# A graph layer with attention and experts: the order of the steps between its two phases is rewritten, and the ring of gathered messages is made six groups deep

## The reference

```python
xn = _layernorm(x)                                   # [6250, 256]
# graph part: 100000 edges sorted by dst, 16 relations
transformed = einsum('ni,rio->rno', xn, weight)      # table of node x relation rows
gnn = segment_sum(transformed[rel_type, src] * norm, dst, num_segments=6250)
# linear attention, 8 heads, softmax of k over the nodes
q, k, v = split(xn @ Wqkv);  k = softmax(k, axis=nodes)
mix = (einsum('nhd,hdv->nhv', q, einsum('nhd,nhv->hdv', k, v)) * gate(xn)) @ Wproj + bproj
x = x + gnn + mix
# 8 experts, the best two of a softmax router, each gelu(t @ w1 + b1) @ w2 + b2
t = _layernorm(x)
return x + t + sum_e combine[:, e] * expert_e(t)
```

## Time and profile before

| what | value |
|---|---|
| median of 3 runs | 1624.4 us (1623.64 to 1628.15) |
| the profiled execution | 1619.85 us |
| its span | 1618.1 us |
| PE busy | 1571.3 us (97%) |
| DVE busy | 1338.5 us (83%) |
| POOL busy | 1010.4 us (62%) |
| ACT busy | 966.3 us (60%) |

### The profile page before, as it was taken

How to read it: one execution, slowest core, us unless ns; L and a number is a source line. 1 busy time by engine, 2 the same in 40 slices (tenths; PEclk the granted TensorE clock), 3 DMA queues, 4 the chain that set the end, 5 groups by cost and what they waited for, 6 DMA issues and landing times.

```text
span 1618.1 us, 31745 instructions
## 1 busy us (share of the span) xinstructions
PE 1571.3 (97%) x10509; PEld 1441.1 (89%) x10509; DVE 1338.5 (83%) x3383; ACT 966.3 (60%) x2161; POOL 1010.4 (62%) x1111
## 2 busy tenths in 40 slices
PE   7999999999999999998779999999999999999998
PEld 6888888888888888886669999999999999999998
DVE  7888665588888888874568999999999999999985
ACT  4454322356556656645457776776767776676764
POOL 5533322677777777737457777777777777777620
PEclk9999999999999999999899999999999999999999
DMA  9777656789888888887233333333333333334320
GB/s 300 263 255 259 232 227 238 242 282 284 286 290 273 288 291 275 286 266 248 88 95 108 105 115 103 112 106 118 105 106 108 107 113 102 112 105 118 105 59 10
DMA packets 127076, 290.50 MB, mean 180 GB/s; under 512 B 21271, under 2 KB 49724, under 8 KB 126914
## 3 DMA queue, kind: packets, MB, share of 16 engines
q1 hardware_dynamic: 86068, 177.19, 29.9%
q0 software_dynamic: 39952, 110.13, 25.2%
q10 hardware_dynamic: 894, 1.16, 0.2%
HBM read 149.49 MB, written 138.90 MB: 178 GB/s over the span
## 4 chain that ended last, share of the span: by engine, by line
PE 90%; DVE 3%; issue 2%; ACT 2%; DMA 1%; POOL 1%; SPq 0%; ACTq 0%; DVEq 0%; POOLq 0%
PE bank L1832 71%; PE bank L2036 4%; PE bank L2037 3%; PE bank L1876 2%; PE bank L1877 2%; PE bank L2032 1%; PE bank L1887 1%; PE bank L1988 1%; PE bank L2076 1%; PE bank L2088 1%; DMA xres<-in_L_gnn_weight 1%; PE bank L1842 1%; DVE pad L1262 1%; PE bank L2085 1%; DMA stg<-table,idxcur 0%
## 5 line engine op out<-in xcount | busy, mean ns | idle before, releaser
L830 POOL DMA_INDIRECT stg<-table,idxcur x495 | 543.1, 1097 | 238.5 <-issue 149.1
L1832 PE MATMUL bank<-wreg,xt 128*128 128x512 f32 x2352 | 578.1, 396 | 0.9 <-DVE wreg L1189 0.4
L1832 PEld LDWEIGHTS bank<-wreg,xt 128*128 128x128 f32 x2352 | 432.9, 188 | 88.8 <-ACT stg L872 1.2
L712 POOL DMA_INDIRECT raw<-table,idxa x297 | 302.2, 1018 | 87.7 <-issue 75.9
L1832 PE MATMUL bank<-tt,wreg 128*128 128x256 f32 (+1 forms) x2400 | 321.9, 284 | 2.7 <-DVE tt L1691 2.7
L1832 PE MATMUL bank<-wreg,ht 128*128 128x256 f32 x2352 | 313.5, 282 | 0.2 <-DVE ht L1741 0.2
L1832 PEld LDWEIGHTS bank<-tt,wreg 128*128 128x128 f32 x2400 | 298.7, 191 | 5.8 <-DVE tt L1691 3.1
L1832 PEld LDWEIGHTS bank<-wreg,ht 128*128 128x128 f32 x2352 | 292.4, 189 | 0.4 <-DVE ht L1741 0.4
L1622 DVE SCALAR_TENSOR_TENSOR ml<-stg,nrm,mh 128x256 fp32r<-128x256 f32 x445 | 190.9, 477 | 15.3 <-ACT mh L1044 15.2
L1237 DVE COPY stg<-bank 128x512 f32<-128x512 f32 x196 | 134.0, 686 | 83.9 <-PE bank L1832 82.7
L1044 ACT ACTIVATE mh<-stg,nrm 128x256 fp32r<-128x256 f32 x445 | 196.4, 499 | 0.3 <-PE bank L2037 0.3
(11 more groups left out here) (248 smaller groups left out, 2317.0 us busy)
## 6 DMA issues: line engine op xcount, KB each, us to landing
table<-stg SPq DMA_DIRECT2D x196, 512.0 KB, 3.6
kv_d<-kvs SPq DMA_DIRECT2D x49, 256.5 KB, 4.9
xt_d<-xt SPq DMA_DIRECT2D x49, 256.0 KB, 4.6
xtp<-xt_d SPq DMA_DIRECT2D x24, 512.0 KB, 3.9
stg<-table,idxcur POOLq DMA_INDIRECT x495, 2.9
sk<-kv_d SPq DMA_DIRECT2D x24, 256.5 KB, 5.5
out_x<-xres SPq DMA_DIRECT2D x24, 256.0 KB
xres<-in_x POOLq DMA_DIRECT2D x23, 256.0 KB, 4.1
```

Source lines behind the costliest of these rows:

```text
L712: pool.indirect_dma_start(ring_a[:, r * EARLY + j, :], None, table[0:LIMIT, :], bass.IndirectOffsetOnAxis(ap=idxa[:, at:at + 1], axis=0)). ...
L830: pool.indirect_dma_start(stg[:, (s % 4) * SUP + j, :], None, table, bass.IndirectOffsetOnAxis(ap=idxcur[:, at:at + 1], axis=0)).then_inc( ...
L1832: mm = pe.matmul(dst, stat(a, c), mov(b, c), start=(n == 0), stop=(n == 3 * chunks - 1))
```

## The change

The ring holds six groups instead of four, packed without gaps (ring_at), with six semaphores, and POOL waits for the sums of the group six earlier. The block of indices holds four half pairs instead of two, and a half pair's indices are copied one step later than before for pair 0. The first four groups are split, and the 16 groups after them stay unsplit (WHOLE_GROUPS). The roots of pair 0 are taken one gather later, those of pair 1 two gathers earlier. The mask of the heads is made in setup, as 128 x 4 numbers, and HEADS reads it as a broadcast. Two semaphores are dropped, and QUERY_ROWS counts on another. The list CHANGE is written anew; the steps in it are the same.

```diff
-    ROOTS, EARLIER_ROOTS = (7, 1), {1: (4, 1), 2: (5, 0)}
+    ROOTS, EARLIER_ROOTS = (7, 1), {1: (4, 2), 2: (4, 1)}
...
+    GROUPS_HELD = 6
...
-        idxcur = sb("idxcur", [P, 4 * (EB - EARLY)], I32, two)
+        idxcur = sb("idxcur", [P, 8 * (EB - EARLY)], I32, two)
...
+        heads = small[:, 52:52 + NB]
...
-        gath = [sem(f"gath{g}") for g in range(4)]
+        gath = [sem(f"gath{g}") for g in range(GROUPS_HELD)]
...
-            return S < WHOLE_GROUPS
+            return WHOLE_GROUPS[0] <= S < WHOLE_GROUPS[1]
-            return tiles_before(S) - tiles_before(WHOLE_GROUPS)
+            first, last = WHOLE_GROUPS
+            return tiles_before(S) - (tiles_before(last) - tiles_before(first) if S >= last else 0)
+
+        def ring_at(S, j):
+
+            return tiles_before(S % GROUPS_HELD) + j
...
-            pool.wait_ge(consts, 10)
+            pool.memset(heads, 1.0).then_inc(consts, 1)
+            pool.wait_ge(consts, 11)
+            pool.affine_select(out=heads, in_=heads, compare_op=ALU.is_ge, fill=0.0, base=0,
+                               pattern=[[-HEAD, NB]], channel_multiplier=1).then_inc(consts, 1)
+            pool.wait_ge(consts, 12)
+            pool.affine_select(out=heads, in_=heads, compare_op=ALU.is_ge, fill=0.0, base=HEAD - 1,
+                               pattern=[[HEAD, NB]], channel_multiplier=-1).then_inc(consts, 1)
             pc = Tally(pool_chain)
 
...
                 n = EB - EARLY
-                at = half * 2 * n
+                at = (2 * i + half) % 4 * 2 * n
                 pool.tensor_copy(idxcur[:, at:at + rows * n].rearrange("p (r e) -> p r e", e=n),
                                  g3[:, bass.ds(4 * i + 2 * half, rows), EARLY:EB]).then_inc(idx_cur, 1)
-
-            def heads():
-                by_head = ctxbd.rearrange("p c (h e) -> p c h e", h=NB)
-                pool.memset(ctxbd, 1.0).then_inc(consts, 1)
-                pool.wait_ge(consts, 11)
-                pool.affine_select(out=by_head, in_=by_head, compare_op=ALU.is_ge, fill=0.0, base=0,
-                                   pattern=[[0, CC], [-HEAD, NB], [0, HEAD]], channel_multiplier=1).then_inc(consts, 1)
-                pool.wait_ge(consts, 12)
-                pool.affine_select(out=by_head, in_=by_head, compare_op=ALU.is_ge, fill=0.0, base=HEAD - 1,
-                                   pattern=[[0, CC], [HEAD, NB], [0, HEAD]], channel_multiplier=-1).then_inc(consts, 1)
 
             pool.wait_ge(flag_ready, 1)
             far = pool.value_load(flag[0:1, 0:1], min_val=0, max_val=NT * P * R)
             first_phase_over(pool)
-            heads()
             next_indices(0, 0, 2)
-            next_indices(0, 1, 2)
             for h in range(PIECES):
                 pool.wait_ge(tbl_st[h], 16 * NT)
...
                 for s in range(groups):
                     if s % 4 == 0:
                         pool.wait_ge(idx_cur, 2 * i + s // 4 + 1)
-                    if s >= 4 or not isinstance(i, int) or i > 0:
-
-                        pool.wait_ge(edge_mm, 8 * i + s - 3)
+                    S = 8 * i + s
+                    if S >= GROUPS_HELD:
+                        pool.wait_ge(edge_mm, S - GROUPS_HELD + 1)
                         apart(pool)
                     for j in range(PART[s % 2]):
                         if (s, j) == EARLIER_ROOTS.get(i, ROOTS) and not (isinstance(i, int) and i < 1):
                             roots2(i - 1, 2)
                         if s % 4 == 3 and j == 1:
                             if s == 3:
-                                if not isinstance(i, int) or i > 0:
-                                    next_indices(i, 1, min(2, groups // 2 - 2))
+                                next_indices(i, 1, min(2, groups // 2 - 2))
                             elif groups == 8:
                                 next_indices(i + 1, 0, 2)
-                        at = s // 2 * n + (s % 2) * CUT + j
+                        at = (4 * i + s // 2) % 8 * n + (s % 2) * CUT + j
                         pool.indirect_dma_start(
-                            stg[:, (s % 4) * SUP + j, :], None, table,
+                            stg[:, ring_at(S, j), :], None, table,
                             bass.IndirectOffsetOnAxis(ap=idxcur[:, at:at + 1], axis=0)
-                            ).then_inc(gath[s % 4], 16)
+                            ).then_inc(gath[S % GROUPS_HELD], 16)
 
             def roots2(p, nt):
...
-                act.wait_ge(gath[s % 4], 16 * n * (2 * i + s // 4 + 1))
+                act.wait_ge(gath[S % GROUPS_HELD], 16 * n * (S // GROUPS_HELD + 1))
                 at = EB * (4 * i + s // 2) + EARLY + (s % 2) * CUT
                 if whole(S):
                     for j in range(n):
-                        m = stg[:, (s % 4) * SUP + j, :]
+                        m = stg[:, ring_at(S, j), :]
                         act.activation(m, m, ACT.Copy, scale=nrm[:, bass.ds(at + j, 1)]).then_inc(msg_hi, 1)
                     return
-                act.wait_ge(edge_mm, S - 1)
+                if S < 2:
+                    act.wait_ge(ctx_mm, HELD)
+                else:
+                    act.wait_ge(edge_mm, S - 1)
                 for j in range(n):
-                    act.activation(mh[:, (s % 2) * CUT + j, :], stg[:, (s % 4) * SUP + j, :], ACT.Copy,
+                    act.activation(mh[:, (s % 2) * CUT + j, :], stg[:, ring_at(S, j), :], ACT.Copy,
                                    scale=nrm[:, bass.ds(at + j, 1)]).then_inc(msg_hi, 1)
...
                 for c in range(CC):
-                    dve.scalar_tensor_tensor(out=ctxbd[:, c, :], in0=bank[5][:, c * P:(c + 1) * P], scalar=rden[:, c:c + 1],
-                                             in1=ctxbd[:, c, :], op0=ALU.mult, op1=ALU.mult).then_inc(ctx_done, 1)
+                    dve.scalar_tensor_tensor(
+                        out=ctxbd[:, c, :].rearrange("p (h e) -> p h e", h=NB),
+                        in0=bank[5][:, c * P:(c + 1) * P].rearrange("p (h e) -> p h e", h=NB), scalar=rden[:, c:c + 1],
+                        in1=heads.unsqueeze(2).to_broadcast([P, NB, HEAD]), op0=ALU.mult,
+                        op1=ALU.mult).then_inc(ctx_done, 1)
 
             def CLEAR():
                 dve.memset(halves(c3[:]), 0.0).then_inc(c3_clear, 1)
...
                         pe.wait_ge(msg_hi, done + j + 1)
-                        mm = pe.matmul(bank[u % 2][:, 0:C], halves(sel[:, m, :]), stg[:, (s % 4) * SUP + j, :],
+                        mm = pe.matmul(bank[u % 2][:, 0:C], halves(sel[:, m, :]), stg[:, ring_at(S, j), :],
                                        start=(s % 2 == 0 and j == 0), stop=(s % 2 == 1 and j == PART[1] - 1))
                         continue
...
                 if isinstance(p, int) and p == 0:
-                    pe.wait_ge(wqc_done, 1)
+                    pe.wait_ge(ctx_done, 2 * CC + 2)
 
                 for v in range(CC):
...
 
-WHOLE_GROUPS = 20
+WHOLE_GROUPS = (4, 20)
 
 
...
 CHANGE = (
-    "HELD_ROWS", "ROWS_OF 0", "FADE", "SELECT 0 0", "SELECT 0 1", "SHIFT 2", "EXP 2", "ROWS_OF 1", "MSGS 0 0", "SUMS 0 0",
-    "ROWS_OF 2", "SHIFT 3", "EXP 3", "MSGS 0 1", "SUMS 0 1", "SELECT 0 2", "ROWS_OF 3", "SHIFT 4", "EXP 4",
-    "MSGS 0 2", "SUMS 0 2", "SHIFT 5", "EXP 5", "ADDS 0 0", "SELECT 0 3", "MSGS 0 3", "SUMS 0 3", "ROWS_OF 4",
-    "SELECT 0 4", "ADDS 0 1", "GELU_TABLE", "MSGS 0 4", "SPLIT 4 0", "SPLIT 4 1", "SELECT 0 5", "ROWS_OF 5",
-
-    "CONTEXT", "SUMS 0 4", "CONTEXT_PE", "MSGS 0 5", "CONTEXT_TURN", "SUMS 0 5", "VALUES", "SELECT 0 6", "HEADS",
-    "QUERY", "MSGS 0 6", "CLEAR", "ADDS 0 2", "QUERY_ROWS", "GATES 0 2", "GATE_ACT 0 2", "SUMS 0 6", "OUT 0 2",
-    "SELECT 0 7", "MSGS 0 7", "SPLIT 5 0", "SUMS 0 7", "SELECT 1 0", "GATE 0 2", "GATE_HI 0 2", "MSGS 1 0", "SUMS 1 0",
-    "ADDS 0 3", "GATE_LOW 0 2", "PROJ 0 2", "SELECT 1 1", "SPLIT 5 1", "MSGS 1 1", "SUMS 1 1", "ADDS 1 0", "STATS 0 2",
-    "SELECT 1 2", "MSGS 1 2", "SUMS 1 2", "SPLIT 6 0", "MEAN 0 2", "NORM 0 2", "SPLIT 6 1", "TURN 0 2", "TURN_HI 0 2",
-    "TURN_LOW 0 2", "MSGS 1 3", "SELECT 1 3", "LAYER1 0 2 0", "LOGIT 0 2", "SUMS 1 3", "LAYER1 0 2 1", "TOP 0 2",
-    "LOW 0 2 0", "ADDS 1 1",
-
-    "WEIGHT 0 2", "SELECT 1 4", "LOW 0 2 1", "SPLIT 7 0", "COMB 0 2", "COMB_HI 0 2", "MSGS 1 4", "LAYER1 0 2 2",
-    "LAYER2 0 2 0", "OUT 1 2", "SUMS 1 4", "GATES 1 2",
-
-    "COMB_LOW 0 2", "SELECT 1 5", "ADD 0 2 0", "LOW 0 2 2", "GATE_ACT 1 2", "GATE 1 2", "LAYER1 0 2 3", "LAYER2 0 2 1",
-    "GATE_HI 1 2", "MSGS 1 5", "SUMS 1 5", "SPLIT 7 1",
-
-    "ADD 0 2 1", "SELECT 1 6", "LOW 0 2 3", "GATE_LOW 1 2", "ADDS 1 2", "LAYER1 0 2 4", "LAYER2 0 2 2", "MSGS 1 6",
-    "SUMS 1 6", "COMBT 0 2",
-
-    "ADD 0 2 2", "SELECT 1 7", "LOW 0 2 4", "COMBT_ACT 0 2", "LAYER1 0 2 5", "PROJ 1 2", "LAYER2 0 2 3", "MSGS 1 7",
-    "SUMS 1 7",
-
-    "ADD 0 2 3", "SELECT 2 0", "LOW 0 2 5", "ADDS 1 3", "LAYER1 0 2 6", "MSGS 2 0", "LAYER2 0 2 4", "SUMS 2 0",
-    "SELECT 2 1", "MSGS 2 1", "SUMS 2 1",
-
```

(50 more changed lines are left out.)

2 lines of the change are left out of this document (removed).

## The result

The changed kernel takes 1605.35 us (median of four runs, 1602.12 to 1607.93) against 1624.77 on the same chip: 0.9876 of it, 95% interval 0.9853 to 0.9899, so 16 to 24 us less. The forecast was 1611, 13 us less. Medians and ratios here leave out runs far slower than the rest of their program's (one of ahead_alone's eight took 3097.78 us).

The account below looks back on a forecast made before the run. PE was taken as the bound, full except for 29.4 us idle around the change of phase. The terms 3.8 + 1.5 + 7.8 sum to 13.1 us, taking the median from 1624.4 to 1611 us; range 1601 to 1621.

Parts of the forecast that it names:

- Slots, 7.8 us: Experts' slots: MSGS ahead of LAYER1 on ACT removes six PE holes, 8.3 us, less a new 0.5; 7.8 us won.
- Head mask, first gather 0.65 us earlier: POOL at the change of phase: mask made in setup, so the first gather goes 0.65 us earlier, not 1.5.
- Front, 3.8 us: Up to LAYER1 0: 2.1 us won before CONTEXT, 2.6 from PROJ 0, less 0.9 for splits; 3.8 us earlier.
- second count: Cross-check: new holes about 21 us for 29.4, 2.7 us less of sums, 2 us shorter cold stretch; 13 us.
- SUMS 1 3 out of the slots, 1.5 us: SUMS 1 3, before placed after LAYER1 0, now lies in PE's holes ahead of it; 1.5 us won.
- Second STATS, 0: After roots(1): PE waits some 5.5 us in three pieces for late gathers, against 2.73 + 2.60 before; 0.
- Steady loop, 0: Repeated pairs after the change of phase: no gain, since PE has no hole there; 0.
- Clock: Around LAYER1 0: TensorE assumed still to fall to 1.2 GHz; a cold stretch 2 us shorter counted only in the cross-check.
- larger: Rival, change of phase: PE stays at 2.4 GHz and the hole before CONTEXT is filled; 1603 us, chance 0.19.
- Smaller: Rival, after roots(1): the gather queue sets the pace and groups come late; price 6 us, 1617 us, chance 0.18.
- Slower: Rival, steady loop: POOL becomes the bound, at 1.30 us a gather losing 21 us; 1632 us, chance 0.07.
- the rule in the Trainium skill: Two-input DVE instructions contend with POOL's SBUF reads: ten gathers 0.13 us slower, 1.3 us on POOL; left out of the sum.

Follow-up runs that it names:

- ahead_alone: Kernel before, with only the messages of five groups scaled ahead of their slot's LAYER1, ring of four kept; 1618.42 us, ratio 0.9966.
- msgs_behind: Changed kernel, with the message scaling of groups 1 6 to 2 2 (five slots) put behind the slot's LAYER1 again; 1611.52 us, ratio 0.9923.
- roots_later: Changed kernel, with POOL's roots of pair 1 put ahead of group 2 6 instead of the second tile of 2 4; 1605.06 us, ratio 0.9900.
- after_again: Changed kernel run once more, unedited, on another chip; 1603.92 us, ratio 0.9900 to the kernel before on that chip.
- turn_list: Changed kernel with the roots as in roots_later, and selections, low halves and messages of groups 2 4 to 2 7 reordered around pair 1's turn; 1599.85 us, ratio 0.9877.
- ring_alone: Kernel before with the ring of six groups and the mask made in setup, but its old list, roots and whole groups; 1620.28 us, ratio 0.9989.
- whole_first: Changed kernel with the first four groups of the phase summed whole again, without low halves on DVE; 1603.60 us, ratio 0.9876.
- better: turn_list with pair 0's roots one gather later, SPLIT 4 0 beside SPLIT 4 1, and SPLIT 7 0 between MEAN and NORM; 1596.91 us, ratio 0.9868.
- split7_behind: Changed kernel with SPLIT 7 0 moved from behind TURN 0 2 to behind LOW 0 2 0; 1604.38 us, ratio 0.9900.

## Why the prediction was right, and where its sizes were off

*Slots, 7.8 us:* right. No hole that ACT's messages end is left, and the new one of 0.5 us that I allowed for did not come; taken out, the order costs 6.8 us. It is the largest single part.

*Head mask, first gather 0.65 us earlier:* 0.42, from POOL's release (1.52 us against 1.94); the store's landing is waited for, as I had it.

*Front, 3.8 us, with CONTEXT at 748.9 behind SPLIT 4 0 and LAYER1 0 at 775.4:* 749.23 and 775.61, the hole before the context 2.77 for 3.5. But the first phase had ended 1.7 us later, so the section gained 5.3; and the same instructions up to LAYER1 0 took 59.1, 60.0, 61.2 and 61.5 us in msgs_behind, roots_later, after_again and turn_list. Five traces average 59.7, against 62.8 in the three with the old front (before, ring_alone and ahead_alone): some 3 us, near my size but not by my way. PE's idle time there is 14.6 us on the mean in the five as in the three, and its work 43.0 in both; what is less is PE's busy time at 1.2 GHz, 4.3 us for 10.4. So what I had won before CONTEXT and by PROJ 0 the new holes took back on the mean (in the first trace they left 2.1 us), and the 3 us are the clock, which I had left as it was. No run has the front's new order alone. The context's hole goes from 2.77 to 5.63 us in the five, and ACT's wait for the landing of group 0 4 stands ahead of it as I wrote; in after_again ACT waits 3.53 us for it, in after 1.43:

```profile
750.82 1.30 ACT L1038 ACTIVATE stg<-stg,nrm 128x256 f32<-128x256 f32 x3 [3.53 <-DMA stg<-table,idxcur]
```

The share I gave to the split itself is not there (whole_first). The 2.7 us less of sums in my second count set the duration of a row (0.51 a tile) against a distance of starts (0.24); by starts the unsplit tile took 0.43, which makes 1.9.

*SUMS 1 3 out of the slots, 1.5 us:* PE's work between LAYER1 0 and the third OUT, half of its busy time at 1.2 GHz taken off, is 46.9 us for 48.6. But the five holes alone move this work too: it is 47.9 with them in msgs_behind and 47.3 without them in ahead_alone. That leaves 0.4 to 0.7 us for SUMS 1 3 (an estimate from these four), less than I gave; it was not tested by itself.

*Second STATS, 0:* the holes from 811 on sum to 5.9 us, those from 827 on before to 6.2, so 0 was right, for a wrong reason. I put them on gathers that come late after the roots; roots_later shows that earlier gathers alone leave them as they are, and turn_list that the list had made them.

*Steady loop, 0:* the term that failed. "PE has no hole there" hid waits too short for a busy share: 0.16 us a pair, 3.2 over 20 pairs (the whole rest behind the third OUT is 2.0 to 2.2 us shorter in the two builds). The row that told of it was POOL's waits for PE; I read them only for whether POOL would become the bound. They fell from 51.5 us in 20 pairs to 0.3.

*Clock:* I allowed 2 us in a second count. 27.3 us at 1.2 GHz became 17.1 in the one trace and 23.9 in the repeat; by PE's busy time in them (22.8, 14.5 and 18.9 us) that is 4.1 and 1.9 us of time.

13.1 forecast, 16.5 and 19.4 measured: up to 3.2 of the difference is the loop, the rest is of the size by which front and clock vary. That the front's 3.8 came near is luck in part, since the clock brought it and not the holes. Of the rivals, *larger* had the number, but neither of its reasons: the clock still fell, if for a shorter time, and the hole before CONTEXT stayed. *Smaller* had the holes, not the cause. *Slower* is refuted: POOL waits 54.8 us for statistics in 20 pairs, 2.7 a pair, and gathers average 1.10 us there as before. From 722 to 740 us thirteen gathers average 1.003 us with five of the new low halves among them, 1.085 before with none: no price can be seen there. In the steady loop there is one: of the changed kernel's 400 gathers from 870 to 1525 us the 208 that have a low half beside them in their first 0.9 us average 1.20 us, the other 192 1.00 (before, 1.25 and 0.98). So the rule in the Trainium skill, SBUF — State Buffer, "Who interferes with whom", that I weighed there agrees with the loop's gathers, though the two sets may differ in more than this. Its price did not reach the time: POOL waits for statistics in these pairs.

## What to carry to other kernels

In a list that each engine follows in order, put the work that the next consumer needs ahead of the work that waits for that consumer; a hole is named by its releaser, but here its cause was what stands ahead of the releaser in the list, and moving the supply earlier (roots_later) did nothing for it. A stretch that shows an engine full can still hold a wait of 0.1 us per turn: compare the period of the loop, and look at who arrives last at its joints. Cut traces at the same instructions, and make two of the same program, before a section of a few us is given to an edit.

## What was not expected of the hardware

Nearly the same work of PE in the change of phase ran at 1.2 GHz for 6.8 us in one program and 41.0 in another, 17.1 and 23.9 in two runs of one. In better the fall at LAYER1 0 lasted for 3.4 us, in after for some 10. The hole before it does not tell which: it was 1.52 us in better and in split7_behind, and there the fall lasted for 10.2. ahead_alone shows what that can cost: 5.1 us of holes taken out, and 3.6 us lost to the clock.
